# A graph network's kernel: GpSimd's indirect DMAs in shorter runs, with waits on TensorE's signals between them

## The reference, cut to what matters

```python
src, dst = edge_index                       # 206250 edges, dst sorted; 6250 nodes, 64 features
h = relu(sage(x, src, dst, W_l1, b_l1, W_r1))       # layer 1, to 128 features
h = relu(sage(h, src, dst, W_l2, b_l2, W_r2))       # layer 2
x = layernorm(x + h @ W_out + b_out)
# where sage(x) = segment_sum(x[src], dst) / max(count, 1) @ W_l + b_l + x @ W_r
out = selu(concat(x[src], edge_attr) @ W1a + b1a) @ W1b + b1b      # one row an edge
mean = segment_sum(out, dst) / max(count, 1)
x = layernorm(x + selu(concat(x, mean, u[0]) @ W2a + b2a) @ W2b + b2b)
```

## Time and profile before

| | us |
|---|---|
| median of 3 runs | 3222.48 (3210.37 to 3230.22) |
| the profiled execution's time | 3233.57 |
| its span | 3231.8 |
| PE busy | 2326.9 (72%) |
| POOL busy | 1802.6 (56%) |
| DVE busy | 1637.4 (51%) |
| ACT busy | 1011.9 (31%) |

### The profile page before, as it was taken

How to read it: one execution, slowest core, us unless ns; L and a number is a source line. 1 busy time by engine, 2 the same in 40 slices (tenths; PEclk the granted TensorE clock), 3 DMA queues, 4 the chain that set the end, 5 groups by cost and what they waited for, 6 DMA issues and landing times.

```text
span 3231.8 us, 54307 instructions
## 1 busy us (share of the span) xinstructions
PE 2326.9 (72%) x19234; PEld 1660.3 (51%) x19234; DVE 1637.4 (51%) x3324; ACT 1011.9 (31%) x2325; POOL 1802.6 (56%) x1854
## 2 busy tenths in 40 slices
PE   2998988877888788526777777777767777775553
PEld 1555555444444344325565655656656555554553
DVE  6988988733344343424444444444444444442332
ACT  4877766500000000122222232223222222222222
POOL 5456666645555555555555555555555555556664
PEclk9999999988889788757788787878787888886665
DMA  7478888445646655223222322223222222222111
GB/s 243 176 219 227 230 220 248 84 96 183 189 132 187 187 161 152 73 51 89 54 54 50 61 51 55 57 50 61 51 55 54 58 56 51 55 52 46 42 43 38
DMA packets 524467, 342.65 MB, mean 106 GB/s; under 512 B 398996, under 2 KB 476495, under 8 KB 520781
## 3 DMA queue, kind: packets, MB, share of 16 engines
q1 hardware_dynamic: 413715, 268.37, 30.5%
q0 software_dynamic: 54240, 57.31, 8.0%
q10 hardware_dynamic: 56250, 13.52, 2.0%
HBM read 201.55 MB, written 137.36 MB: 105 GB/s over the span
## 4 chain that ended last, share of the span: by engine, by line
PE 32%; another core or an unknown queue 30%; issue 14%; DVE 10%; ACT 7%; POOL 4%; DVEq 1%; ACTq 1%; DMA 0%; POOLq 0%
PE agg_ps L1572 9%; PE cnt_ps L1443 4%; PE agg_ps L1715 4%; POOL A_sb L1010 4%; DVE arena L1898 3%; PE agg_ps L1449 2%; PE agg_ps L1450 2%; ACT A_sb L1102 2%; PE cnt_ps L1666 1%; ACT A_sb L1256 1%; DVEq L2253 1%; DVE arena L2274 1%; ACT A_sb L1277 1%; PE u_ps L1701 1%
## 5 line engine op out<-in xcount | busy, mean ns | idle before, releaser
L1010 POOL DMA_INDIRECT A_sb<-source_terms,src_cur x1092 | 1040.7, 953 | 811.1 <-issue 282.0
L964 POOL DMA_INDIRECT sorted_edges<-pm_row,pm_to x520 | 560.9, 1079 | 389.8 <-DVE pm_to L2032 221.3
L1572 PE MATMUL agg_ps<-A_sb,arena 128*128 128x448 f16 x1911 | 425.6, 376 | 51.9 <-issue 51.4
L1898 DVE TENSOR_TENSOR arena<-iota_code,arena 128x2048 f16<-128x2048 f16 (+1 forms) x392 | 435.3, 1175 | 49.0 <-PE cnt_ps L1443 46.2
L1102 ACT ACTIVATE A_sb<-cnt_ps 128x392 f32 (+1 forms) x784 | 385.5, 498 | 174.0 <-PE cnt_ps L1443 107.7
L1715 PE MATMUL agg_ps<-pm_row,A_sb 128*65 128x192 f32 x896 | 221.7, 404 | 189.7 <-DVE A_sb L2255 170.5
L1443 PE MATMUL cnt_ps<-arena 128*128 128x98 f16 x3136 | 285.5, 215 | 69.7 <-ACT A_sb L1102 39.2
L1277 ACT ACTIVATE A_sb<-u_ps 128x256 f32<-128x256 f32 x169 | 65.0, 384 | 846.9 <-remote 764.0
L1443 PEld LDWEIGHTS cnt_ps<-arena 128*128 128x128 f16 x3136 | 194.4, 101 | 260.4 <-issue 199.0
L1572 PEld LDWEIGHTS agg_ps<-A_sb,arena 128*128 128x128 bf16 x1911 | 191.6, 102 | 256.1 <-issue 119.0
L1674 PE MATMUL agg_ps<-A_sb 128*65 128x48 f32 x2184 | 194.7, 236 | 134.5 <-issue 68.7
(11 more groups left out here) (313 smaller groups left out, 3563.0 us busy)
## 6 DMA issues: line engine op xcount, KB each, us to landing
counts_matrix<-A_sb SPq DMA_DIRECT2D x12, 5488.0 KB
A_sb<-counts_matrix SPq DMA_DIRECT2D x12, 5488.0 KB
arena<-in_edge_attr_dram SPq DMA_DIRECT2D x90, 256.0 KB
sorted_edges<-zrow SPq DMA_DIRECT2D x13, 1716.0 KB
arena<-sorted_edges SPq DMA_DIRECT2D x169, 128.0 KB
A_sb<-source_terms,src_cur POOLq DMA_INDIRECT x1092
overlapping_rows<-A_sb SPq DMA_DIRECT2D x1, 13056.0 KB, 39.4
A_sb<-in_edge_attr_dram SPq DMA_DIRECT2D x46, 256.0 KB
```

Of the source, the lines that this page charges most:

```text
L964: pool.indirect_dma_start(out=sorted_d, out_offset=bass.IndirectOffsetOnAxis(ap=pm_to[:, k, j:j + 1], axis=0), in_=pm_row[:, k, j, :], in_ ...
L1010: pool.indirect_dma_start(out=gath[k][:, j * F:(j + 1) * F], out_offset=None, in_=p_d, in_offset=bass.IndirectOffsetOnAxis(ap=src_cur[k][: ...
L1572: ins = pe.matmul(agg_ps[:, 0:SBN], Hsb[:, part, blk, :], Asb(half)[:, blk, :], start=False, stop=(part == 2), skip_group_check=True)
L1898: ins = dve.tensor_tensor(hot_rows[:, slots], iota_code[:, 0:n, :].unsqueeze(1).to_broadcast([P, AT_ONCE * SUB // 2, n, 2]), turned[:, bas ...
```

## The change

In layer 2, from block 1 on, POOL stops before a group's fourth and its seventh scatter (`STOP_AT`) and waits for a signal of PE: which one is laid down by the group's place i in its block (`first_stop`, `second_stop`). In a block of three groups these are, in order, `h2_turned`, `o_ready`, `x2_turned`, `agg2_ready`, and `hT_turned` and `v2_ready` of the next block; in a block of four the first group waits for `v2_ready` and `h2_turned`, the second for `o_ready` alone, the last two as in a block of three. In the edge stage the gathers of a slot of two steps stop once more, before the seventh, for the unit product of the slot's second step (`unit_z`). What is computed, the data that move, and the queues they move on stay as they are.

```diff
--- before.py
+++ after.py
@@ -129,6 +129,7 @@
 STEPS = UNITS + SUM_STEP
 HOT_RING = 3
 AT_START = 3
+STOP_AT = (3, 6)
 FIRST_STEP = 4
 LAST_STEP = NEGC - 26
 
@@ -951,8 +952,33 @@
             gather_windows(4)
             gather_fine(5 * SETS, 6 * SETS)
             split_h(0)
+            def first_stop(s, i):
+                if i == LAYER2[s] - 1:
+                    if s < NSB - 1:
+                        pool.wait_ge(hT_turned, s + 1)
+                elif i == LAYER2[s] - 2:
+                    pool.wait_ge(x2_turned, s)
+                elif LAYER2[s] == 3:
+                    pool.wait_ge(h2_turned, s)
+                elif i == 0:
+                    pool.wait_ge(v2_ready, s)
+                else:
+                    pool.wait_ge(o_ready, s)
+
+            def second_stop(s, i):
+                if i == LAYER2[s] - 1:
+                    if s < NSB - 1:
+                        pool.wait_ge(v2_ready, s + 1)
+                elif i == LAYER2[s] - 2:
+                    pool.wait_ge(agg2_ready, s + 1)
+                elif LAYER2[s] == 3:
+                    pool.wait_ge(o_ready, s)
+                elif i == 0:
+                    pool.wait_ge(h2_turned, s)
+
             def scatter(q):
                 k = q % PRING
+                s = max([s for s in range(1, NSB) if FIRST[s] <= q], default=0)
                 if q == 0:
                     pool.wait_ge(pm_blank, PM_BLANK + 32)
                 if q == 2 * RG:
@@ -961,6 +987,10 @@
                     pool.wait_ge(pm_blank, PM_BLANK + 16 * (NR - 2))
                 pool.wait_ge(pm_rows, PM_ROWS + q + 1)
                 for j in range(EJ):
+                    if j == STOP_AT[0] and s > 0:
+                        first_stop(s, q - FIRST[s])
+                    if j == STOP_AT[1] and s > 0:
+                        second_stop(s, q - FIRST[s])
                     pool.indirect_dma_start(
                         out=sorted_d, out_offset=bass.IndirectOffsetOnAxis(ap=pm_to[:, k, j:j + 1], axis=0),
                         in_=pm_row[:, k, j, :], in_offset=None).then_inc(pm_gone[k], 16)
@@ -1003,20 +1033,22 @@
             pool.wait_ge(edges_in, ENDS_IN)
             pool.wait_ge(p_stored, 16 * NSB)
 
-            def gather(g, k, width=EJ, paced=False):
+            def gather(g, k, width=EJ, steps=()):
                 for j in range(width):
-                    if paced and j == AT_START:
+                    if len(steps) == 2 and j == AT_START:
                         pool.wait_ge(z_ready, g)
+                    if len(steps) == 2 and j == 2 * AT_START and 2 <= steps[1] < UNITS + 2:
+                        pool.wait_ge(unit_z, UNIT_Z + steps[1] - 1)
                     pool.indirect_dma_start(
                         out=gath[k][:, j * F:(j + 1) * F], out_offset=None, in_=p_d,
                         in_offset=bass.IndirectOffsetOnAxis(ap=src_cur[k][:, j:j + 1], axis=0)).then_inc(gath_in[k], 16)
 
-            def gather_next(g, k, width=EJ, paced=False):
+            def gather_next(g, k, width=EJ, steps=()):
                 pool.wait_ge(z_made, g - DEEP + 1)
                 pool.wait_ge(idx_made, g + 1)
                 pool.wait_ge(seg_ready, g - 2)
                 pool.sem_inc(pool_at, 1)
-                gather(g, k, width, paced)
+                gather(g, k, width, steps)
 
             pool.iota(iota_p, [[1, PWIN]], 1, 0, allow_small_or_imprecise_dtypes=True).then_inc(unit_set, 1)
             for i in range(2):
@@ -1025,7 +1057,7 @@
                 pool.wait_ge(idx_made, k + 1)
                 gather(k, k)
             for g in range(DEEP, NEGC):
-                gather_next(g, g % DEEP, edges_of(g), len(SLOT_STEPS[g - 2]) == 2)
+                gather_next(g, g % DEEP, edges_of(g), SLOT_STEPS[g - 2])
 
             pool.wait_ge(flagB, 1)
             left = pool.value_load(flag_i[0:1, 1:2], min_val=0, max_val=1)
```

## The result

The kernel before took 3216.43 us (median of 4 runs), the changed one 3123.57 us (3107.51 to 3132.62, 4 runs): a ratio of **0.9721**, 95% interval 0.9686 to 0.9756, or 93 us. The forecast was 3050 with a range of 2985 to 3155: faster, as said, but little more than half the 172 us, and outside the forecast's own range of 2985 to 3100. Executions profiled: 3233.57 before, 3124.13 after, 109 us apart.

A forecast was written before the change was run, and what follows sets the result against it. Bound: chains of waits, with TensorE's signals held behind POOL's back-to-back indirect DMAs. Edge slots 136 plus layer 2 36 gives 172 us off 3222.5: 3050 us, 8-in-10 range 2985 to 3155, own range 2985 to 3100 (chance 0.60).

The forecast's parts named there:

- The mechanism: Both stages: two or three back-to-back indirect DMAs by POOL hold TensorE's signals until about 1.1 us after the run.
- Slot A: Edge slot of two unit steps after a slot of one: 13.07 us becomes 12.15, saving 0.92 in each of 39.
- Slot B: The other edge slots of two unit steps: 15.96 us becomes 13.2, saving 2.76 in each of 25.
- Slot C keeps its run of eight: Edge slots of one unit step: eight gathers stay one run, the next group's wait shortens, saving 0.76 in each of 41.
- the edge sum: Edge slots: savings of 36, 69 and 31 us over the three slot kinds, 136 us together.
- Layer 2: Scatter stops shorten 12 blocks from 566 to 530 us, a gain of 36, between 0 and 86.
- `pm_to` waits: Layer 2: POOL's 6.3 us waits for DVE, one left in each block of three groups, none in four.
- Rival 2: Edge slots: POOL sets the pace, A and C keep their length, only B gains; 3117 to 3153 us, chance 0.12.
- Rival 1: Only the edge slots gain; in layer 2 POOL is the bound and passes most stops; 3086 us, chance 0.14.
- Rival 3: The stops don't stop: TensorE's signal comes in a run's first two DMAs and is sent at once; 3222 us, chance 0.06.
- Rival 4: Held signals are let go only after the group's eighth DMA, so stops cost time; 3326 us, chance 0.05.
- The page beside it: Skill page on matmul signals, without any part for GpSimd: by it signals are not 4 us late and stops lose time.

The follow-up runs named there:

- the small kernel: Separate kernel without the computation: engines post signals beside GpSimd DMA runs of 1 to 16; latest TensorE signal 1.1 us (run of 8), 10.95 us (16).
- c_stop: Changed kernel plus, in slots of one unit step, a POOL wait for `z_ready` before the fourth gather; 0.9524 of the kernel before, 3095 us.
- c_own: Changed kernel plus, in slots of one unit step, a POOL wait for its own three landed gathers before the fourth; 0.9445 of the kernel before, 3068 us.
- fours_one: `c_own` without the scatters' second stop in layer 2's four blocks of four groups; 1.0241 of the kernel before, which takes 2544 us on that chip.

## Why the prediction was right and where it failed

- **The mechanism** stands for chips like the one predicted on. Behind runs of three ACT starts 1.3 us (A) and 0.9 us (B) after the second product on average, against 4.3 and 4.1 before, a pause on POOL's own landing does the same, and the small kernel shows lateness only beside unbroken runs of eight or more indirect DMAs. That three in a row are enough is the edge slots' alone; the small kernel does not show it. The limit that no row of before could show: on a chip without the hold there is nothing for the stops to give back, and the kernel before is 670 to 705 us faster there.
- **Slot A**: 13.12 to 12.33, 0.79 saved against 0.92. Right.
- **Slot B**: 16.41 to 13.86, 2.55 against 2.76. Right. The 15.96 that the prediction read from one B is 0.45 below the mean of the 25; its 1462 + 10 met the 1473 of the window only because that window ends one C early (all slots are 1476 + 10).
- **"Slot C keeps its run of eight"** is the step that failed. I moved POOL 2.7 us forward in B and ended B with "next group 1692.75", the usual 0.3 behind the last gather, and the same in A, and did not ask what stood behind that gap. In the trace of before a C begins after 2.33 us of idleness, and that pause was what kept its run at eight. Taking it away joined 2 and 8. C lost 1.53 us in place of gaining 0.76: 41 x 2.29 = 94 us of the 103 by which the edge sum (136) missed (33). `c_stop` and `c_own` give it back, C at 12.3.
- **Layer 2** was mis-sized the other way: 71 us, where I took 36 between bounds of 0 and 86; the blocks come to 494 us where I had 530. `pm_to` waits came out as I had them (48 us against 8 x 6.3 = 50). The stops did not: 76 at 1.0 us each were 76 us in the sum, and 23 waits of 2.4 us, 56 us in all, in the trace; the rest passed. That is 20 of the 36 us. Some 12 more is an error of form: my 530 was built from POOL's work and waits, and the same account of before (40 groups x 10.1 + 173 = 577) is 12 above the 565 measured, so model should have been set against model.
- **Rival 2**'s time (3117 to 3153) held the result, and its mechanism did not: A got shorter, and more pauses made C shorter still. **Rival 1** had the stages swapped, though POOL passed most of layer 2's stops (57 of 80), as it said. **Rival 3** is out: all 64 new stops of the edge slots paused POOL, for 1.1 us each. **Rival 4** is out too: signals came behind runs of three, and the time is 3124, not 3326. The page beside it: the Trainium skill ("Perfetto Trace Analysis", Per-engine timelines) lets the matmul's semaphore update follow PSUM's acknowledgement. On the chip of `fours_one` the trace agrees (0.04 us to ACT's start), on the others it does not (7.1 us at 1576.02 of the changed kernel).
- The two errors, -103 and +35, cancel in part: 172 - 68 = 104, and the profiled executions differ by 109. The stated range held by luck more than by working: it reached to rival 2's slow end, while the forecast's own range was missed.

## What to carry to other kernels

When a pause goes away, ask what it was separating: a shorter wait in one slot can weld two bursts of another engine's work together. Where TensorE's signals come late beside long runs of indirect DMAs on GpSimd, break the runs by waits on signals of TensorE: none of these paused POOL on the chip without the hold, where a wait for its own landed gathers still cost 1.8 us each, and in layer 2 such a wait cost 3.1 us on average and up to 9.5. Judge a wait by its total over all releasers, not by the name that the profile gives it.

## What the runs showed of the hardware

- Chips differ in whether signals are held: the same kernel took 3249, 3248 and 3213 us on three chips and 2544 on a fourth, where ACT starts 0.04 us after TensorE's product beside runs of 24. Why is open, and so is whether the recording of the profile has a part in it; the profiled execution of the changed kernel took 3124.13 us among 3107.51 to 3132.62.
- Where they are held, it takes indirect DMAs issued by GpSimd back to back. One to six made TensorE's signals at most 0.27 us late in the small kernel, ten 4.1, sixteen 10.95; plain DMAs, or pauses in between, at most 0.12. VectorE's and ScalarE's signals were not late beside a run of eight. What makes runs of three and five enough in the edge slots is open.
- PE's own products are spaced out as well, by 0.6 and 1.1 us of "issue" in the run of ten shown.
- The profile of such a chip can lack semaphore events (25 for 40 signals of ScalarE), so a missing event is not a late signal; the start of the engine that waits tells.
